# The chain of dt moved ahead in the orders of ScalarE, GpSimd and the SyncE queue of a decoder layer's scan

## The reference

```
z, xv, Bm, Cm, dt_in = split(x @ in_proj_w.T)       # 1024, 256, 256, 1024, 128 columns
dt  = softplus(dt_in @ dt_proj_w.T + dt_proj_b)     # 1024 channels
dA  = exp(dt[..., None] * A)                        # 16 states for each channel
dBx = (dt * x_full)[..., None] * Bg
h   = dA_i * h + dBx_i                              # over the 512 tokens, in order
y   = sum over the states of C_i * h
out = (y + D_skip * x_full) * silu(z) @ out_proj_w.T
```

## Time and profile before

| | us |
|---|---|
| median of the runs | 2795.44 |
| profiled execution, its own time | 2799.06 |
| its span, first to last instruction | 2797.3 |
| TensorE busy | 2618.7 (94%) |
| VectorE busy | 2082.0 (74%) |
| GpSimd busy | 1285.8 (46%) |
| ScalarE busy | 1191.1 (43%) |
| chain that ended last, TensorE's share | 66% |

### The profile page before, as it was taken

The page is one execution under the profiler, slowest core; times in us unless marked ns, Lnnn a source line. Parts: engine busy times, 40 slices in busy tenths (PEclk is TensorE's granted clock), DMA queues, the critical chain, the costliest instruction groups (busy, mean ns, idle before and its releaser), DMA issues.

```text
span 2797.3 us, 32656 instructions
## 1 busy us (share of the span) xinstructions
PE 2618.7 (94%) x11152; PEld 1877.7 (67%) x11160; DVE 2082.0 (74%) x2656; ACT 1191.1 (43%) x1786; POOL 1285.8 (46%) x868
## 2 busy tenths in 40 slices
PE   7888888898889879999999999999999999999999
PEld 4443444454345337888888778788878788888887
DVE  5999899999999976543376677777877865555553
ACT  5655555555555635422254543343333422222221
POOL 4899899899999961210001023123222422222220
PEclk9999899899899879999999999999999999999999
DMA  7754655555465437121111112112111121111111
GB/s 248 220 165 129 180 150 139 166 158 148 125 182 160 132 113 266 54 76 53 62 51 61 40 44 69 46 46 68 46 39 46 45 53 46 51 48 50 49 46 68
DMA packets 152311, 275.37 MB, mean 98 GB/s; under 512 B 27344, under 2 KB 27856, under 8 KB 151632
## 3 DMA queue, kind: packets, MB, share of 16 engines
q1 hardware_dynamic: 152144, 273.27, 32.7%
HBM read 178.01 MB, written 61.34 MB: 86 GB/s over the span
## 4 chain that ended last, share of the span: by engine, by line
PE 66%; DVE 9%; issue 8%; POOL 8%; ACT 4%; DMA 3%; SPq 1%; POOLq 0%; DVEq 0%; ACTq 0%
PE ps L1757 19%; PE ps L1759 19%; PE ps L1758 19%; DVE state L1401 4%; POOL read L1233 4%; PE ps L1806 3%; PE ps L1822 3%; ACT ps L896 1%; DMA vpack<-vl 1%; DMA b_d<-ev 1%; PE ps L1966 1%; POOL dt_t L1197 1%; POOL sp_rest L1182 1%; PE ps L1940 1%; DMA uraw<-y_d 1%
## 5 line engine op out<-in xcount | busy, mean ns | idle before, releaser
L1233 POOL TENSOR_TENSOR read<-state,c_t 128x512 f32<-128x512 f32 x512 | 662.9, 1316 | 74.4 <-DVE state L1401 35.8
L1401 DVE TENSOR_TENSOR_SCAN state<-ps,drive 128x512 f32<-128x512 f32 x512 | 622.5, 1216 | 4.2 <-ACT ps L896 1.7
L1295 POOL TENSOR_TENSOR wdeq<-packed,scales 128x1024 f32<-128x1024 f16 x96 | 256.2, 2668 | 800.7 <-DVE packed L1530 800.7
L1757 PE MATMUL ps<-xh,ghi 128*128 128x512 f32 x1536 | 607.3, 395 | 0.0
L1759 PE MATMUL ps<-xh,glo 128*128 128x512 f32 x1536 | 598.0, 389 | 0.0
L1758 PE MATMUL ps<-xl,ghi 128*128 128x512 f32 x1536 | 597.8, 389 | 0.0
L896 ACT ACTIVATE ps<-ps,a_exp 128x512 f32<-128x512 f32 x512 | 337.2, 661 | 385.4 <-PE ps L1806 383.9
L1392 DVE TENSOR_TENSOR drive<-ps,b_t 128x512 f32<-128x512 f32 x512 | 344.2, 672 | 53.6 <-PE ps L1806 49.5
L1697 DVE TENSOR_TENSOR act_o<-act_o,ps 128x512 f32<-128x512 f32 x192 | 131.8, 686 | 284.6 <-PE ps L1759 283.2
L1153 ACT ACTIVATE ahi<-act_o 128x512 fp32r<-128x512 f32 x192 | 121.6, 633 | 520.6 <-DVE act_o L1697 520.6
L1757 PEld LDWEIGHTS ps<-xh,ghi 128*128 128x128 f32 x1536 | 288.4, 188 | 62.6 <-issue 3.1
(11 more groups left out here) (197 smaller groups left out, 3842.0 us busy)
## 6 DMA issues: line engine op xcount, KB each, us to landing
whi<-w_d SPq DMA_DIRECT2D x63, 256.0 KB, 4.9
wlo<-w_d SPq DMA_DIRECT2D x63, 256.0 KB, 5.5
b_d<-ev SPq DMA_DIRECT2D x32, 256.0 KB
dpack<-dh SPq DMA_DIRECT2D x64, 128.0 KB, 4.4
dpack<-dl SPq DMA_DIRECT2D x64, 128.0 KB, 2.3
b_t<-b_d SPq DMA_DIRECT2D x32, 256.0 KB, 5.4
vpack<-vh SPq DMA_DIRECT2D x64, 128.0 KB, 2.3
vpack<-vl SPq DMA_DIRECT2D x64, 128.0 KB, 2.4
```

What stands on the lines that cost most here:

```text
L1233: pool.tensor_tensor(read[:, n % RRING, :], state[:, n % SRING, :], c_t[:, g % 2, :], ALU.mult).then_inc(read_ready, 1)
L1295: pool.tensor_tensor(wdeq[:, :].rearrange("p (h n) -> p h n", h=2), codes, scale, ALU.mult).then_inc(deq, 1)
L1401: dve.tensor_tensor_scan(state[:, n % SRING, :], ps[:, decay_bank(n), :], drive[:, n % DRING, :], 0.0, ALU.mult, ALU.add)\
L1757: pe.matmul(out_, w_h, x_h, start=(start and k == 0), stop=False)
```

## The change

Five things move, and no operation is added or taken away.

On the SyncE queue the packs of step g+1 stand ahead of `weights_after(first + 1)`. On ScalarE dh of step g+1 moves from slot 6 to 2, vh from slot 8 to 4, and softplus of step g+2 from slots 12 to 15 to slots 11 to 14. On GpSimd rest and sum of a step move from slots 0 and 1 of the step before it to slots 14 and 15 of the step before that (for step 1 they stay in slot 0 of step 0), dt from slot 2 to 0, dt_x from 3 to 1, dt_low from 7 to 3, v_low from 9 to 5.

```diff
                 if g >= 1:
                     store_y(g - 1)
-                if jobs:
-                    weights_after(first + 1)
                 if 0 <= g + 1 < STEPS:
                     load_pack_dt(g + 1)
                     load_pack_v(g + 1)
+                if jobs:
+                    weights_after(first + 1)
                 if jobs:
                     spill(first + 1)
...
                     if 0 <= g + 1 < STEPS:
-                        if c == 6:
+                        if c == 2:
                             dt_high(g + 1)
-                        if c == 8:
+                        if c == 4:
                             v_high(g + 1)
                     if nb < B:
+                        if c == 11:
+                            soft_abs(g + 2)
                         if c == 12:
-                            soft_abs(g + 2)
+                            soft_pos(g + 2)
+                            soft_exp(g + 2)
                         if c == 13:
-                            soft_pos(g + 2)
+                            soft_one(g + 2)
                         if c == 14:
-                            soft_exp(g + 2)
-                        if c == 15:
-                            soft_one(g + 2)
                             soft_log(g + 2)
...
+                    if g == 0 and c == 0:
+                        soft_rest(1)
+                        soft_sum(1)
                     if g + 1 < STEPS:
                         if c == 0:
-                            soft_rest(g + 1)
+                            soft_dt(g + 1)
                         if c == 1:
-                            soft_sum(g + 1)
-                        if c == 2:
-                            soft_dt(g + 1)
+                            dt_x(g + 1)
                         if c == 3:
-                            dt_x(g + 1)
-                        if c == 7:
                             dt_low(g + 1)
-                        if c == 9:
+                        if c == 5:
                             v_low(g + 1)
+                    if g + 2 < STEPS:
+                        if c == 14:
+                            soft_rest(g + 2)
+                        if c == 15:
+                            soft_sum(g + 2)
```

## The result

The changed kernel has a median of 2818.68 us (2817.45 to 2820.92), the kernel before, run beside it, 2796.23: a ratio of 1.0080, 95% interval 1.0063 to 1.0098. It is slower by 22.4 us where 13.0 were forecast; 2818.68 lies inside the stated range. The profiled executions say 2817.45 and 2799.06 for themselves, 18.4 us apart.

The account below looks back on a forecast made before the run. VectorE (94% busy) and GpSimd (93%) were taken as nearly full in the scan, with lateness where engines' orders cross. Losses of 25.1 us less 12.1 gained gave +13.0 on 2795.44, so 2808.4 us; range 2790 to 2832.

Parts of the forecast that it names:

- The path: Scan 14, five GpSimd operations, dt, its copy dh, next step's scan 3: at least 10.11 us, where 8.55 sufficed before.
- The twenty stretches: Scan 14 to next scan 3, steps 6 to 29 without 10, 11, 18, 19: 188.77 to 202.2 us, +13.4.
- the second owlo: Step 30: a second subtraction of the output weights on GpSimd, between read 14 and dt, delays scan 3: +3.8 us.
- the first rival: The shortage doesn't reach VectorE, which needs dt 1.55 us earlier; only gains are left: 2781 us, chance 0.12.
- The four stretches left out at 0: Scan 14 to scan 3 in steps 10, 11, 18, 19: VectorE's extra work already makes them over 10.11 us, cost 0.
- The weight tile: Slot 8 of steps 7, 15, 23: TensorE's wait for a late tile goes as SyncE issues earlier, 12.1 us gained.
- both halves of the change matter: Claim that the 12.1 us at slot 8 needs both the new SyncE order and the earlier producers.
- part is regained: Step 0: scan 3 at 66.7 instead of 62.93, part recovered because ScalarE is the late one there: +3.0 us.
- The subtractions beside GpSimd: Six VectorE subtractions of two SBUF operands in slots 14 and 15 meeting more GpSimd work: 0, between 0 and 5 us.
- The slow starts: First slots of a step wait as TensorE's clock falls in slots 12 to 15: up to 1.51 us, called untouched.
- The clock rival: TensorE stalls at slot 5 and its clock falls there too, in 14 more steps: +21, 2829 us, chance 0.10.
- the signs named for a wrong forecast: No idle at slot 3, a clock of 0.50 in the middle of steps, or the weight wait still there.

Follow-up runs that it names:

- e3: Changed kernel with the SyncE order of before (second weight tile ahead of the packs): median 2814.12 us, ratio 1.0052.
- e2: Kernel before with only the SyncE part of the change (packs ahead of the second weight tile): median 2814.56 us, ratio 1.0058.
- e1: Changed kernel with only ScalarE's two copies two slots later (dh in slot 4, vh in slot 6): median 2794.94 us, ratio 0.9985.
- e10: Changed kernel with each spread matmul issued twice in slots 12 to 15 and in all slots of steps without projections: median 2811.34 us, ratio 1.0042.
- e8: Kernel before with each spread matmul issued twice in slots 12 to 15 and in all slots of steps without projections: median 2790.11 us, ratio 0.9974.
- e4: Changed kernel with dt one slot earlier on GpSimd, right behind the sum: median 2806.0 us, ratio 1.0027.
- the mended order: Changed kernel with the old SyncE order, dh and vh in slots 4 and 6 (6 and 8 in steps 0 and 30): median 2792.92 us, ratio 0.9981.

## Why the prediction was right, and where it was off

**The path.** It held within a few hundredths: dt starts 7.45 to 7.52 us after scan 14 in 18 of the 20 plain steps (7.53 worked out), the stretch 328.78 - 321.28 = 7.50 is one of them, and scan 3 follows at 10.10 (10.11). In the other two, steps 12 and 20, dt starts at 7.83 and 7.82, behind the step in which VectorE has its extra work. The twenty stretches took 202.35 us (202.2). Step 30 is 3.91 us longer (3.8): its chain waits behind the second owlo, as said. The waits stand where they were looked for, idle time ahead of scan 3 and 4 us at dh. The condition of the first rival, dt 1.55 us earlier, was not met. The four stretches left out at 0 moved by +0.3, -0.4, +0.8 and -0.4 us.

**The weight tile.** Forecast 12.1 us, measured 20.01 - 7.88 = 12.1. The size was right and a part of the reason wrong: "both halves of the change matter" fell with e3 and e2. The moves on GpSimd and ScalarE do it alone, and the queue's order alone does harm. The failed step is the count along the queue: v's last half, 6.5 us sooner as worked out (15.3 against 21.8 us into the step), was counted through the new order only, and the same count through the old one, one weight tile ahead of the packs, would have given the tile in time as well.

**Steps 0 to 5 were mis-sized.** Forecast 7.9 us in all, measured 9.8. Step 0 is 5.3 us longer (3.0) and step 1 2.3 (0.95); steps 4 and 5 are 2.3 longer (2.9) and step 3 not at all (1.0). In step 0 "part is regained" was an assumption without a row. The timeline of step 0:

```profile
61.29 1.27 POOL L1233 TENSOR_TENSOR read<-state,c_t 128x512 f32<-128x512 f32 x1 [11.81 <-DMA c_t<-c_d]
62.52 1.29 POOL L1182 TENSOR_TENSOR sp_rest<-sp_abs,sp_exp 128x512 f32<-128x512 f32 x1
63.95 1.29 POOL L1188 TENSOR_TENSOR sp_log<-sp_log,sp_rest 128x512 f32<-128x512 f32 x1
65.32 1.26 POOL L1197 TENSOR_TENSOR dt_t<-sp_log,sp_pos 128x512 f32<-128x512 f32 x1
...
66.61 0.63 ACT L872 ACTIVATE dh<-dt_t 128x512 fp32r<-128x512 f32 x1 [5.95 <-POOL dt_t L1197]
```

Here rest, sum and dt follow one another, each on the one before, and are 1.43 and 1.37 us apart, not 1.245: dt stands 4.03 after read 0 where 3.7 was counted. VectorE then idles 5.87 us ahead of scan 3, which comes 12.0 us after the first scan instead of 8.2. These 3.8 us are the delay that was worked out; of them 0.8 were to come back, and another 1.4 were lost in slots 3 to 15 instead.

**The subtractions beside GpSimd.** I priced them at 0, between 0 and 5. The group by line over the scan, before and after:

```profile
L1376 DVE TENSOR_TENSOR wlo<-wraw,whi 128x512 fp32r<-128x512 f32 x16 | 14.8, 922 | 0.0
```

```profile
L1380 DVE TENSOR_TENSOR wlo<-wraw,whi 128x512 fp32r<-128x512 f32 x16 | 17.5, 1096 | 0.0
```

2.7 us of busy time more, inside my bounds and above the value taken. It came mostly in other slots than those I counted. Slots 14 and 15 hold five such subtractions, not six, and only those of steps 0 and 1 got longer (0.67 to 1.52 and to 1.48). The larger part is in slot 3, which I had left out: 0.67 to 1.77 us in step 0, to 1.83 in step 1 and to 1.84 in step 4. Others got shorter, as 1.62 to 0.67 in slot 7 and 1.22 to 0.67 in slot 11 of step 0. Each passes into the slot's length whole: slots 3, 7, 11 and 15 of step 0 changed by +1.10, -0.95, -0.56 and +0.86 us. So the subtractions are 0.45 of the 5.3 us of step 0 and 1.45 of the 2.3 us of step 1, which is what step 1 was mis-sized by. In slot 15 of step 0 the meeting can be seen, before and after:

```profile
89.87 0.67 DVE L1376 TENSOR_TENSOR wlo<-wraw,whi 128x512 fp32r<-128x512 f32 x1
90.03 1.66 POOL L1233 TENSOR_TENSOR read<-state,c_t 128x512 f32<-128x512 f32 x1 [0.41 <-DVE state L1401]
```

```profile
95.11 1.28 POOL L1182 TENSOR_TENSOR sp_rest<-sp_abs,sp_exp 128x512 f32<-128x512 f32 x1
...
95.41 1.52 DVE L1380 TENSOR_TENSOR wlo<-wraw,whi 128x512 fp32r<-128x512 f32 x1
```

Before, the subtraction began first and took 0.67 us; GpSimd's product began 0.16 later and took 1.66, where 1.28 to 1.30 is usual. In the change `soft_rest` has begun 0.30 us ahead, and the subtraction ends at 96.93, 0.54 us after `soft_rest` (96.39) and 1.52 after its own start. The Trainium skill, "SBUF — State Buffer", section "SBUF: two separate sides", says that whichever of the two starts first holds the shared ports for the whole of its instruction. The trace agrees with 0.67 against 1.52 us. The shares in steps 0 and 1 are read from these lengths; no run took the meetings away alone.

**The slow starts were not "untouched".** This is the step that failed in its wording, though it cost little here: slot 0 gave 1.6 us back. What it did cost was part of the forecast of e1: there I took away a shortage and counted its full 13.4 us, and the starts took back 3.6.

**The clock rival was right in a small part.** Steps 13 and 29 are 2.6 and 2.3 us longer, 1.2 and 0.9 of it at slot 8. These are steps without projections, and there the rival's account fits. From scan 5 to scan 8 and from scan 8 to scan 9 of step 13, before and after (columns as in rows 6):

```profile
476.15:481.28 5.13, 3.68 (x3) 0.69 0.36 102
481.28:483.71 2.43, 1.23 (x1) 0.94 0.00 0
```

```profile
486.35:491.49 5.14, 3.62 (x3) 0.50 0.76 195
491.49:495.07 3.58, 1.21 (x2) 0.57 0.58 141
```

The granted clock is 0.50 in the middle of steps 5, 13, 29 and 30, one of the signs named for a wrong forecast; before it was 0.60 to 0.75 there. So the clock fell in steps without projections before the change, too, and not in slots 12 to 15 alone, as the prediction has it. The rival priced this at 21 us, in 14 steps. Some 2 came: with the spreads twice (e10) slot 8 of steps 13 and 29 is on time. (At slot 8 of step 21, 3.60 and 3.58 us, nothing changed.) e10 also shows that the clock had no part in the 10.1 us of the path. The Trainium skill, "TensorE: Matmul & The Clock Gate", section "HAM oscillation — how this bites in real kernels", describes matmul bursts that start at half clock after each wait, in every round. The trace agrees for the start of a step: slot 0 costs 21.1 us in the kernel before and 6.3 in e8, whose TensorE has more to do ahead of it. Nearly all of the change's loss was elsewhere.

**The sum for the profiled pair.** Forecast 13.0, measured 18.4. Of the 5.4 between them 3.0 lie before step 6 (9.8 + 1.1 against 7.9; the 1.1 is the first scan, which varies by more than that) and 2.1 at slot 8 of steps 13 and 29. All the rest, losses and gains, leaves 0.3. The other 4 us, between 18.4 and the 22.4 of the medians, are the distance of single executions from their medians. The closeness in the two main terms is no luck: 13.4 against 13.6 and 12.1 against 12.1, each with the wait that was named.

## What to carry to other kernels

When a step is moved along several engines' orders, write down for each move the path that feeds it and the slot in which the engine needs it. Here dt moved by two slots and its consumer by four, and an in-order engine then waits with all that stands behind it. The move from slot 2 to 1 cost 1.7 us a step, that from 3 to 2 less, since slow starts covered part of it, and the right place was worth more than the whole loss of 22 us without any other edit. A queue's order should be costed with the old producers too, since here the producers alone gave the gain. And two waits that cover each other must be removed together: the mended order alone gave 0.2%, busy spreads alone 0.3%, both 1.0%.

## What the runs showed of the hardware

A kernel that is nearly full on VectorE and GpSimd can lose its time in TensorE's clock: the same eight gathers took 1.93 us with the granted clock at 0.50 and 1.06 at 1.00. Two matmuls for one in the last four slots of a step, and in all slots of steps without projections, brought slot 0 from 21.1 to 6.3 us; three for one cost more than they gave (2780.1 against 2771.4). A VectorE subtraction of two SBUF operands took 0.67 us where it began first and 1.52 where GpSimd had begun 0.30 us ahead of it, and its slot got longer by the whole difference. GpSimd's 128x512 operations started 1.245 us apart with an independent one in between, and 1.34 to 1.39 (31 times in e4) where one needs the result of the one just ahead.
